# A V projection in another loop order: tokens on the partitions, weights loaded again for each group of token tiles

## The reference

```
def _L0_attn_ref(x, wq, wk, wv, out_w, out_b):
    q = x @ wq.T
    k = x @ wk.T
    v = x @ wv.T                       # the change touches this product
    q = _apply_rope_full(q)
    k = _apply_rope_full(k)
    ...                                # 16 heads of 64, scores, softmax
    out = jnp.einsum('bhqk,bhkd->bhqd', attn, v)
    return out @ out_w.T + out_b

x = x + _L0_attn_ref(_layernorm(x), wq, wk, wv, out_w, out_b)
x = x + _L0_ffn_ref(_layernorm(x), rail_maker, rail_up_proj, w_cproj)
```

## Time and profile before

| | us |
|---|---|
| median of 3 runs | 3173.78 |
| lowest, highest | 3172.71, 3178.57 |
| profiled execution, its own time | 3173.51 |
| its span, slowest core (core 7) | 3172.0 |
| its fastest core (core 4) | 3138.0 |
| TensorE busy, core 7 | 2375.4 |
| ScalarE busy | 1055.3 |
| VectorE busy | 720.5 |
| GpSimd busy | 236.4 |

### The profile page before, as it was taken

How to read it: one execution, slowest core, us unless ns; L and a number is a source line. 1 busy time by engine, 2 the same in 40 slices (tenths; PEclk the granted TensorE clock), 3 DMA queues, 4 the chain that set the end, 5 groups by cost and what they waited for, 6 DMA issues and landing times.

```text
span 3172.0 us, 33427 instructions; the slowest of 8 cores (3138.0 to 3172.0 us)
## 1 busy us (share of the span) xinstructions
PE 2375.4 (75%) x8094; PEld 853.1 (27%) x8094; DVE 720.5 (23%) x1675; ACT 1055.3 (33%) x1967; POOL 236.4 (7%) x449
## 2 busy tenths in 40 slices
PE   0248600743899999999889975979797979798989
PEld 0013200210112222222122221434343434343434
DVE  3310287122444444444412220000000000000000
ACT  1322201101566666666411116323232323233310
POOL 0012100113111111111000000000000000000000
PEclk9999855765555555555555555999898999899999
DMA  1122100126444444444022223889898889888898
GB/s 34 60 34 27 20 0 0 14 34 108 93 91 94 89 95 93 95 89 92 17 70 76 74 65 95 275 257 275 241 271 240 271 254 276 259 270 272 268 283 274
DMA packets 318424, 439.53 MB, mean 139 GB/s; under 512 B 55072, under 2 KB 173856, under 8 KB 318240
## 3 DMA queue, kind: packets, MB, share of 16 engines
q1 hardware_dynamic: 245504, 365.01, 37.8%
q0 software_dynamic: 61216, 47.22, 11.7%
q10 hardware_dynamic: 11520, 25.17, 2.1%
HBM read 425.73 MB, written 58.72 MB: 153 GB/s over the span
## 4 chain that ended last, share of the span: by engine, by line
PE 56%; DMA 17%; DVE 10%; ACT 7%; issue 6%; SPq 2%; POOL 1%; DVEq 1%; ACTq 0%; POOLq 0%
PE pf L1032 19%; DMA wcs<-wcb 14%; PE po L738 8%; PE ps L662 8%; PE pat L887 7%; PE pqk L380 4%; PE pf L982 3%; PE pc L788 3%; PE pqk L494 2%; DMA bbuf<-blkB 2%; ACT ebuf L696 1%; DVE pbuf L716 1%; SPq L960 1%; SPq L976 1%; DVE scrW L427 1%
## 5 line engine op out<-in xcount | busy, mean ns | idle before, releaser
L1032 PE MATMUL pf<-wcs,Hb 128*128 128x512 bf16 x4096 | 1010.7, 385 | 165.4 <-DMA wcs<-wcb 163.8
L995 ACT ACTIVATE Hb<-pf 128x256 bf16<-128x256 f32 x1024 | 393.4, 384 | 737.9 <-PE pf L982 708.6
L1032 PEld LDWEIGHTS pf<-wcs,Hb 128*128 128x128 bf16 x4096 | 394.5, 99 | 595.1 <-issue 235.4
L738 PE MATMUL po<-pbuf,Vx 128*65 128x512 bf16 x559 | 353.2, 633 | 44.9 <-DVE Ost L797 44.5
L662 PE MATMUL ps<-QT,KT 64*128 64x512 bf16 x559 | 336.6, 604 | 9.9 <-ACT ebuf L696 8.5
L982 PE MATMUL pf<-btb,w2b 128*128 128x256 bf16 x1024 | 288.8, 289 | 37.0 <-issue 14.5
L1049 DVE TENSOR_TENSOR ob<-pf,xr 128x512 f32<-128x512 f32 x32 | 22.1, 692 | 1252.2 <-PE pf L982 903.6
L703 ACT ACTIVATE ebuf<-ps,cpool 128x512 bf16<-128x512 f32 x303 | 208.2, 687 | 139.6 <-PE ps L662 114.4
L887 PE MATMUL pat<-owt,Ost 64*128 64x512 bf16 x512 | 224.1, 629 | 20.7 <-DMA owt<-owT 20.7
L696 ACT ACTIVATE ebuf<-ps,cpool 128x1024 bf16<-128x1024 f32 x128 | 142.6, 1114 | 132.3 <-PE ps L662 106.8
L592 POOL DMA_DIRECT2D wcv<-wcT x256 | 135.1, 528 | 593.9 <-DMA wcb<-wcv 579.2
(11 more groups left out here) (97 smaller groups left out, 1212.7 us busy)
## 6 DMA issues: line engine op xcount, KB each, us to landing
wcs<-wcb SPq DMA_DIRECT2D x1024, 256.0 KB, 5.1
wcv<-wcT POOLq DMA_DIRECT2D x256, 128.0 KB, 3.1
wcb<-wcv SPq DMA_DIRECT2D x256, 128.0 KB, 1.7
w2b<-w2scr SPq DMA_DIRECT2D x256, 128.0 KB, 3.6
xin<-x SPq DMA_DIRECT2D x16, 512.0 KB, 4.0
xrb<-x SPq DMA_DIRECT2D x16, 512.0 KB, 4.8
xres<-xnw ACTq DMA_DIRECT2D x16, 512.0 KB, 5.0
xr<-xres SPq DMA_DIRECT2D x16, 512.0 KB, 6.7
```

The source lines that it names most:

```text
L738: P.op("tensor", (lambda b_=pbi, f2=hf, kc_=kc, h_=h, pb_=pob, f_=first, l_=last: (lambda e: e.matmul(po[pb_][0:65, :], Vx[:, 1040 * kc_ + ...
L995: P.op("scalar", (lambda m_=mc, z_=zb, p_=p: (lambda e: e.activation(Hb2[p_][:, SB2 * m_:SB2 * (m_ + 1)], pf[z_][:, 0:SB2], AF.Gelu, bias= ...
L1032: P.op("tensor", (lambda m_=mc, s_=sl2, e_=e2, pi=pb_i, i_=i, p_=p: (lambda e: e.matmul(pf[pi][:], Hb2[p_][:, SB2 * m_ + 128 * s_:SB2 * m_ ...
```

## The change

V is computed with tokens on the partitions. For each group `g` of two token tiles (256 tokens), and within it for each feature chunk `e8`, POOL loads a whole 128x1024 block of V's weights into a buffer, and TensorE does four products with it: two token tiles by two halves of 512 output features. `At` is now the stationary operand and the weights are the moving one. The four banks are then evicted by ACT straight into `Vx`, 8 heads each. The transposes, `vts` and DVE's copies are gone from this stage. The two weight buffers now take turns from one `e8` to the next, and each is free again after its four products. All 8 blocks are loaded again for each of the 8 groups.

```diff
-    for vq in range(4):
-        wi = vq % 2
+    for g in range(8):
         for e8 in range(8):
-            P.op("gpsimd", ... out=wqb[i_][:, 256 * e_:256 * (e_ + 1)],
-                in_=wvT_d[128 * e_:128 * (e_ + 1), 256 * q_:256 * (q_ + 1)])
-                 waits=[wqb_free[wi]] if e8 == 0 else (), inc=f"dw{wi}")
-        ev_w = P.now(f"dw{wi}")
-        for d2 in range(2):
-            dvch = 2 * vq + d2
-            for e8 in range(8):
-                for sc in range(4):
+            i = e8 % 2
+            P.op("gpsimd", ... out=wqb[i_][:, 0:1024],
+                in_=wvT_d[128 * e_:128 * (e_ + 1), :])
+                 waits=[wqb_free[i]], inc=f"dw{i}")
+            ev_w = P.now(f"dw{i}")
+            for s2 in range(2):
+                sl = 2 * g + s2
+                for dv2 in range(2):
+                    bk = s2 * 2 + dv2
                     wts = [ev_w, ev_At]
                     if e8 == 0:
-                        wts.append(bank_free[sc])
-                        pqk[s_][:],
-                        wqb[i_][:, 256 * e_ + 128 * d_:256 * e_ + 128 * (d_ + 1)],
-                        At[:, S * e_ + 512 * s_:S * e_ + 512 * (s_ + 1)],
-                         waits=wts if e8 == 0 else (), inc="t")
+                        wts.append(bank_free[bk])
+                        pqk[b_][:],
+                        At[:, S * e_ + 128 * s_:S * e_ + 128 * (s_ + 1)],
+                        wqb[i_][:, 512 * d_:512 * (d_ + 1)],
+                         waits=wts, inc="t")
+            wqb_free[i] = P.now("t")
-            for sc in range(4):
-                P.op("scalar", ... activation(vts[v_][:, 512 * s_:512 * (s_ + 1)], pqk[s_][:], AF.Copy)
-                     waits=[ev_mm, vts_free[vb]], inc="s")
-            emit_transposes(vts[vb], NSL, ... Vx ..., [ev_vts, ones_evt], (pbt2A, pbt2B), vst)
-        wqb_free[wi] = last_mm
+        for s2 in range(2):
+            for dv2 in range(2):
+                P.op("scalar", ... activation(Vx[... 8 heads of 64, 65 apart ...], pqk[b_][:], AF.Copy)
+                     waits=[ev_mm, ones_evt], inc="s")
+                bank_free[bk] = P.now("s")
```

More of the change, by code:

```diff
@@ L473, in build_nc @@
     ones_evt = P.now("v")
-    vst = {}
-    vts_free = [None, None]
-    for vq in range(4):
-        wi = vq % 2
+    for g in range(8):
         for e8 in range(8):
-            P.op("gpsimd", (lambda q_=vq, e_=e8, i_=wi: (lambda e: e.dma_start(
-                out=wqb[i_][:, 256 * e_:256 * (e_ + 1)],
-                in_=wvT_d[128 * e_:128 * (e_ + 1), 256 * q_:256 * (q_ + 1)])))(),
-                 waits=[wqb_free[wi]] if e8 == 0 else (), inc=f"dw{wi}")
-        ev_w = P.now(f"dw{wi}")
-        last_mm = None
-        for d2 in range(2):
-            dvch = 2 * vq + d2
-            vb = dvch % 2
-            for e8 in range(8):
-                for sc in range(4):
+            i = e8 % 2
+            P.op("gpsimd", (lambda e_=e8, i_=i, g_=g: (lambda e: e.dma_start(
+                out=wqb[i_][:, 0:1024],
+                in_=wvT_d[128 * e_:128 * (e_ + 1), :])))(),
+                 waits=[wqb_free[i]], inc=f"dw{i}")
[4 more added lines that the diff above has]
+                    bk = s2 * 2 + dv2
@@ L491, in build_nc @@
                     wts = [ev_w, ev_At]
                     if e8 == 0:
-                        wts.append(bank_free[sc])
-                    P.op("tensor", (lambda i_=wi, e_=e8, d_=d2, s_=sc: (lambda e: e.matmul(
-                        pqk[s_][:],
-                        wqb[i_][:, 256 * e_ + 128 * d_:256 * e_ + 128 * (d_ + 1)],
-                        At[:, S * e_ + 512 * s_:S * e_ + 512 * (s_ + 1)],
-                        start=(e_ == 0), stop=(e_ == 7))))(),
-                         waits=wts if e8 == 0 else (), inc="t")
@@ L500, in build_nc @@
-            ev_mm = P.now("t")
-            last_mm = ev_mm
-            for sc in range(4):
-                P.op("scalar", (lambda s_=sc, v_=vb: (lambda e: e.activation(
-                    vts[v_][:, 512 * s_:512 * (s_ + 1)], pqk[s_][:], AF.Copy,
-                    bias=0.0, scale=1.0)))(),
-                     waits=[ev_mm, vts_free[vb]], inc="s")
[L507 to L514, removed]
@@ L515, in build_nc @@
-            vts_free[vb] = P.now("t")
-        wqb_free[wi] = last_mm
+                        wts.append(bank_free[bk])
+                    P.op("tensor", (lambda e_=e8, s_=sl, d_=dv2, i_=i, b_=bk: (lambda e: e.matmul(
+                        pqk[b_][:],
+                        At[:, S * e_ + 128 * s_:S * e_ + 128 * (s_ + 1)],
+                        wqb[i_][:, 512 * d_:512 * (d_ + 1)],
+                        start=(e_ == 0), stop=(e_ == 7))))(),
+                         waits=wts, inc="t")
@@ new lines, in build_nc @@
+            wqb_free[i] = P.now("t")
+        ev_mm = P.now("t")
+        for s2 in range(2):
+            sl = 2 * g + s2
+            for dv2 in range(2):
+                bk = s2 * 2 + dv2
+                h0 = 8 * dv2
+                P.op("scalar", (lambda s_=sl, b_=bk, h_=h0: (lambda e: e.activation(
+                    Vx[:, 1040 * s_ + 65 * h_:1040 * s_ + 65 * h_ + 520].rearrange(
+                        "p (a b) -> p a b", a=8)[:, :, 0:64],
+                    pqk[b_][:].rearrange("p (a b) -> p a b", a=8),
+                    AF.Copy, bias=0.0, scale=1.0)))(),
+                     waits=[ev_mm, ones_evt], inc="s")
+                bank_free[bk] = P.now("s")
```

## The result

| | before | after |
|---|---|---|
| median of 10 runs, us | 3181.29 | 3227.74 |
| profiled execution, its own time | 3173.51 | 3227.09 |
| its span, slowest core (7 in both) | 3172.0 | 3225.5 |
| V's stage on core 7, last memset to first `ba` | 139.3 | 197.2 |
| the same, mean of the 8 cores | 136.0 | 193.9 |

The ratio is 1.0148, with a 95% interval of 1.0116 to 1.0179, or +37 to +57 us. The forecast was +45 us. (The ratio leaves disturbed executions out, so it is not quite that of the medians.) The two profiled executions differ by more, 53.6 us, since the one before lies 7.8 us under its median.

A forecast was written before the change was run, and what follows sets the result against it. V's stage was taken as bound by its load loop's latency: 27 turns of 6.50 us plus the ends give 184.2 us against 139.1, so 3173.5 + 45 = 3219 us; range 3186 to 3262.

The forecast's parts named there:

- What bounds V's stage: V's stage, 139.1 us behind the rotary work, alone changes length; everything later sits behind a barrier and moves equally.
- The loop: Each V weight buffer cycles through load, landing, four products, next issue: 6.50 us for two blocks, latency-bound, not bandwidth-bound.
- the signs named: Expected in V's stage: TensorE waits some 3 us every second block or more, over 100 us total; stage 184 us.
- Its terms: One buffer turn in V's stage: landing 3.8 us, hop to TensorE 0.24, four products 1.92, hop to POOL 0.54.
- the 184.2 of the sum: V's stage: last block's products end at 180.7 us after 27 turns, then final evictions and hops, giving 184.2 us.
- The sum of the kernel: Whole kernel: V's stage grows by 45.1 us, so 3173.5 + 45 = 3219 us.
- The clock: TensorE in V's stage was expected at half clock, 0.50, with 1.7 us of products in each 3.25.
- the two cases: V's stage at half clock, +45.1 us, or at full clock, +20.2 us; full or mixed clock had chance 0.23.
- The covers: Evictions between V's groups were to hide behind the next block's landing, with 1.2 us spare a group, adding nothing.
- The late landing: Rival: V's weight loads land in 5.3 us, a turn takes 8.0, +86 us, 3259 us; chance 0.18.
- The faster loop: Rival: V's load loop beats the transposes, landing 2.4 us at full clock, -17 us, 3156 us; chance 0.05.
- the price: V's stage breaks even at a landing of 3.05 us at full clock, or 2.1 us at half clock.

The follow-up runs named there:

- experiments 1 and 2: Changed kernel with four weight blocks in flight, ratio to the kernel before 0.9919; changed kernel with V's weights loaded once and kept, ratio 0.9803.
- Experiment 4: Changed kernel loading only 512 of each V weight block's 1024 columns, used for both output halves; ratio to the kernel before 1.0090, stage 159.4 us.
- Experiment 3: Changed kernel with three extra, unread products behind each block's four; ratio to the kernel before 1.0123, V's stage 169.2 us.

## Why the prediction was right

**What bounds V's stage.** Right. In the mean of the cores the stage grew by 57.9 us and the whole span by 58.8. On single cores the other stages did more than move, by -23 to +14 us.

**The loop.** Right in kind, which experiments 1 and 2 show from both sides: more blocks in flight cut the stage to 116.5 us, none needed cut it to 74.1. The DMA engines at 52% of their time match the 1.6 to 1.9 us for each 3.25. Of the signs named, one was a little off: TensorE waits before nearly every block, 1.6 us in the mean (94.8 us over 59 waits), not some 3 before every second and over 100 in total.

**Its terms.** Landing 4.35 for 3.8, the hop to TensorE 0.14 for 0.24, products 1.86 for 1.92, the hop to POOL 0.54 as taken. The mis-sized term is the landing, and by the prediction's own sign (a median of 3.5 to 4.1 us) it was wrong on core 7, at 4.3, though not on cores 2 to 5. I had it as `wcv`'s 3.1 us plus 0.6 to 0.9 of engine time. Experiment 4 shows 0.8 to 1.0 us for the second half of the bytes on cores 2 to 5, which is the upper of my two figures; the engines were busy 1.9 us for each load in the changed kernel (52.3% of 197 us over 54). The other 0.3 us on cores 0, 1, 6 and 7 stays open.

On core 7, from the end of group 1's second block, at 545.87 + 4.18 = 550.05, to the last one, at 738.62, 27 turns took 6.98 us each for 6.50. That makes 13 us, the difference between the stage's 197.2 and the 184.2 of the sum. The 27 landings of the chain are 4.37 us each in the mean, 15 us more than at 3.8. The hop to TensorE and the products gave 4 us back. The other 2 us are a crossing that the prediction had at nothing, told under the covers.

**The sum of the kernel.** +45 was forecast and the ratio says +47, partly by luck: the stage itself grew by 58 us in the profiles, 13 more than forecast. On core 7 4 us of it came back elsewhere, and the profiled execution before lies 8 us under its median, which the ratio doesn't see.

**The clock.** Right: 0.53 in the stage. On core 7 it is 0.81 from 549 to 560 us and 0.51 from 560 to 738. Experiment 3 took it to 0.97 and gained 20 us where the landings were equal, where the prediction had set 45 - 20 = 25 us between the two cases. The rule of the Trainium skill weighed for this ("TensorE: Matmul & The Clock Gate", section "HAM oscillation — how this bites in real kernels") tells of short runs of matmuls between waits for a DMA that each start at the low clock. The trace agrees in the low clock, but the page's loop waits 3 to 5 us for each DMA and this one 1.6 in the mean, and at 0.51 its clock hardly came back at all between them.

**The covers.** The evictions between the groups were not quite free. The prediction had the two blocks of a turn 1.7 us apart; they came 3.3 to 3.6 us apart around 596 and 2.6 to 4.2 around 620, so that the next group's first block could land before ACT had freed the banks. Its four products took 2.46 us from 571.97, 2.14 from 599.79 and 2.46 from 626.93, for 1.87 without such a wait. On core 7 this entered the chain only once, since the chain mostly ran through the other buffer:

```profile
651.66 1.88 PE pqk L490 x4
657.90 4.16 DMA wqb<-wvT
```

Between these two lies an eviction from 653.67, and the next buffer's products behind it. By what the other terms leave over, it cost an estimated 2 us. The pitch of 65 costs ACT nothing (2.68 us for 2.66 before), and the loads under the rotary work delayed nobody: DVE's last memset started at 544.90, where it was 545.77.

**The rivals.** The late landing was the direction of the error, but at 4.35 us, not 5.3; only with four in flight was it 5.7. The faster loop needed a landing under 3.05 us and full clock. Even half the bytes landed in 3.1, and experiment 3 had the clock without the landing: neither alone is enough, as the price said.

The rule of the Trainium skill for a transfer issued by GpSimd ("DMA: Bandwidth & Descriptors", section "Anatomy of one DMA — SWDGE (gpsimd) path"), 2.0 us plus the bytes at 436 GB/s, was too low both times: an estimated 3.2 us for a measured 4.3, and 2.6 for 3.1 in experiment 4.

## What to carry to other kernels

When a loop order makes an operand travel again, reckon the round trip of its buffer (landing, use, release, next issue) and divide by the blocks in flight: here 6.9 us for two blocks of four products each, whatever the DMA engines could carry. The landing itself grows when more are in flight: 5.7 us with four, for 4.3 with two. Here four products, 1.9 us, stood against a landing of 4.3, and the low clock came on top. Before judging a new order by its time, take the reload out: the same order was 2% faster than the old kernel with its weights kept in the buffers that it had itself set free, and 4.6% faster under work that left its engines idle.

## What was unexpected

- Extra products that nobody reads made V's stage 17 to 23 us shorter on the cores whose landings stayed the same, by lifting the granted clock from 0.53 to 0.97.
- The landing of the same loads differs by core: in the changed kernel 3.9 to 4.1 us on cores 2 to 5 and 4.3 on cores 0, 1, 6 and 7, and the stage goes with it, 187.1 to 192.7 against 197.0 to 198.6 us. It is not fixed to the cores: in experiment 3 the medians were 3.8 to 4.0 us on all eight. No run here tells why.
- From 128 KB to 256 KB written, the landing rose by 0.8 to 1.2 us (3.1 to between 3.9 and 4.3), from 64 KB to 128 KB not at all (3.4 and 3.1).
